# Fewer tiles projected ahead of the attention loop, the rest as side steps, and joined query DMAs

## What is computed

```python
q = split_heads(x @ wq.T) * qk_scale
k = split_heads(x @ wk.T) * qk_scale
v = split_heads(x @ wv.T)
q, k = (_rope(q), _rope(k))
energy = jnp.einsum('bhtd,bhld->bhtl', q, k) + mask
attn = jax.nn.softmax(energy, axis=-1)
out = jnp.einsum('bhtl,bhld->bhtd', attn, v)
```

## Time and profile before

| what | us |
|---|---|
| median of 3 runs | 2142.7 (2142.36 to 2144.84) |
| the profiled execution's own time | 2145.87 |
| its span, first to last instruction | 2144.1 |
| PE busy in the span | 1853.9 (86%) |
| DVE busy | 1308.9 (61%) |
| ACT busy | 975.8 (46%) |
| POOL busy | 798.0 (37%) |

### The profile page before, as it was taken

One profiled execution on the slowest core, in us unless ns is written; L12 is line 12 of the kernel. 1 busy time (PEld: TensorE's weight loads), 2 busy tenths in 40 slices (PEclk: granted clock), 3 DMA queues, 4 the chain that ended last, 5 costly groups with the idle time before them and its releaser, 6 DMA issues. The chain is left out here.

```text
span 2144.1 us, 38575 instructions
## 1 busy us (share of the span) xinstructions
PE 1853.9 (86%) x12834; PEld 1660.0 (77%) x12834; DVE 1308.9 (61%) x2935; ACT 975.8 (46%) x2165; POOL 798.0 (37%) x983
## 2 busy tenths in 40 slices
PE   5899999999999999999999995521669999999980
PEld 4688888888888888888888884511669999999980
DVE  5466654577663677663667743677856565666645
ACT  2244344344343444444443442243546666666646
POOL 3242043431142431243431101000656666766643
PEclk9799999999999999999999997555789999999995
DMA  4443134333234432234432211300024444544419
GB/s 113 113 105 99 53 99 110 99 103 95 65 96 111 105 103 81 73 92 116 102 96 78 69 50 47 136 0 0 1 79 134 152 144 156 152 154 144 147 32 313
DMA packets 189208, 215.24 MB, mean 100 GB/s; under 512 B 26672, under 2 KB 154664, under 8 KB 184964
## 3 DMA queue, kind: packets, MB, share of 16 engines
q1 hardware_dynamic: 173188, 203.12, 31.3%
q0 software_dynamic: 15872, 10.24, 2.9%
HBM read 129.66 MB, written 56.62 MB: 87 GB/s over the span
## 5 line engine op out<-in xcount | busy, mean ns | idle before, releaser
L572 PEld LDWEIGHTS out_ps<-v_sb,probs 128*128 128x128 f32 x4352 | 565.3, 193 | 20.8
L572 PE MATMUL out_ps<-v_sb,probs 128*128 128x65 f32 x4352 | 573.9, 271 | 0.0
L784 DVE TENSOR_REDUCE part_max<-rows_ps 128x1 f32<-128x512 f32 (+2 forms) x576 | 346.6, 618 | 183.3 <-PE rows_ps L531 113.2
L686 ACT ACTIVATE probs<-scores_ps 128x512 f32<-128x512 f32 (+3 forms) x640 | 329.4, 537 | 152.4 <-PE scores_ps L559 76.6
L1566 PE MATMUL up_ps<-xe_t,w 128*128 128x320 f32 x1920 | 289.7, 311 | 1.7 <-DVE xe_t L1673 1.7
L1566 PEld LDWEIGHTS up_ps<-xe_t,w 128*128 128x128 f32 x1920 | 284.6, 189 | 2.2 <-issue 1.9
L555 PE MATMUL scores_ps<-q,k_st 128*128 128x512 f32 (+2 forms) x640 | 272.9, 426 | 2.8 <-ACT probs L686 1.3
L528 PE MATMUL rows_ps<-k_st,q 128*128 128x512 f32 (+3 forms) x640 | 249.5, 404 | 22.2 <-DMA q<-q_low_cols 10.3
L960 POOL TENSOR_TENSOR products<-qk,cos_sin 128x256 f32<-128x256 f32 x236 | 169.5, 751 | 241.8 <-ACT qk L653 241.8
L556 PE MATMUL scores_ps<-q,k 68*128 68x512 f32 (+2 forms) x640 | 236.0, 369 | 0.0
L1529 POOL DMA_INDIRECT acc_rows<-out_rows,token x96 | 148.7, 1549 | 128.7 <-ACT out_rows L1656 117.4
(11 more groups left out here) (276 smaller groups left out, 2731.5 us busy)
## 6 DMA issues: line engine op xcount, KB each, us to landing
w_raw<-in_w_expert SPq DMA_DIRECT2D x32, 1536.0 KB, 6.3
k<-k_st SPq DMA_DIRECT2D x160, 128.0 KB, 2.3
k_st<-parts SPq DMA_DIRECT2D x128, 128.0 KB, 2.4
q<-q_up_cols SPq DMA_DIRECT2D x128, 128.0 KB, 2.8
w_raw<-in_w_adapter SPq DMA_DIRECT2D x32, 384.0 KB, 6.9
x_t<-in_x_t SPq DMA_DIRECT2D x64, 128.0 KB, 2.3
q_up_cols<-parts SPq DMA_DIRECT2D x64, 128.0 KB, 2.4
q_low_cols<-parts SPq DMA_DIRECT2D x64, 128.0 KB, 2.4
```

The source lines that it names most:

```text
L572: mm = pe.matmul(o_ps[:, u % 2, s * (HD + 1):(s + 1) * (HD + 1)], probs[:, g % P_RING, s * P:(s + 1) * P], v_sb[:, place(b, j), h, :], sta ...
L686: act.activation(probs[:, g % P_RING, low:CH], s_ps[:, g % S_RING, low:CH], ACT.Exp).then_inc(exp_done, 1)
L784: red = dve.tensor_reduce(to, r_ps[:, e % R_RING, 0:width], AX.X, ALU.max, negate=g == 0)
```

## The change

`FIRST` becomes 6, and all six rotations of the opening are DVE's. Tiles 6 and 7 become side steps of the loop: their inputs are loaded and split in the opening (`FIRST_X` = 8), their projections stand in slots 0 and 2, their rotation on POOL, their transposes in slots 4 and 6; the tiles behind them move to later slots, and the plan allows a tile's split only once the values of the tile two ahead are projected. The maxima of the fifth unit (the first that needs tiles 4 to 7) move from slots 1 to 8 to slots 8 to 12. The weight splits for the later projections go from behind tile 1 to the front of DVE's listing, and POOL no longer waits for the weights before its first split. In SP's listing two loads more stand ahead of each store. The two query stores of a tile are one DMA, and the two copies of a unit's upper queries are loaded by one DMA, whose source names the 64 rows twice.

```diff
-FIRST = 8
-FIRST_ON_POOL = (1, 4, 7)
+FIRST = 6
+FIRST_X = FIRST + 2
...
+        if n < FIRST_X:
+            project_at[n] = 2 * (t - FIRST)
+        elif b == 0:
+            project_at[n] = 4 + 9 * (t - 8) // 2 if t < 12 else 22 + 9 * (t - 12)
...
-                for part_, to in enumerate(("q_up", "q_low")):
-                    sp.dma_start(dram[to][:, :, n * P:(n + 1) * P].rearrange("h d t -> d h t"),
-                                 raw(parts[0:HD, n % 2, part_])).then_inc(qk_stored[n % 2], 16)
+                sp.dma_start(dram["q"][:, :, :, n * P:(n + 1) * P].rearrange("a h d t -> d a h t"),
+                             raw(parts[0:HD, n % 2])).then_inc(qk_stored[n % 2], 16)
...
-                for to in (q1[0:HD, r], q1[HD:P, r]):
-                    sp.dma_start(raw(to), dram["q_up"][h, :, tokens]).then_inc(q_loaded[r], 16)
-                sp.dma_start(raw(q2[0:HD, r]), dram["q_low"][h, :, tokens]).then_inc(q_loaded[r], 16)
+                sp.dma_start(raw(q1[:, r]), dram["q"][0, h, :, tokens].unsqueeze(0).to_broadcast([2, HD, CH]))\
+                  .then_inc(q_loaded[r], 16)
+                sp.dma_start(raw(q2[0:HD, r]), dram["q"][1, h, :, tokens]).then_inc(q_loaded[r], 16)
...
-            for n in range(2, FIRST + 2):
+            for n in range(2, FIRST_X):
                 load_xt(n)
-                if n >= 4:
-                    store_qk(n - 4)
+                if n >= 5:
+                    store_qk(n - 5)
             for u in range(HEADS):
+                if FIRST_X - 5 + u < FIRST:
+                    store_qk(FIRST_X - 5 + u)
                 load_q(u)
                 load_k2(u)
-                if u < 2:
-                    store_qk(FIRST - 2 + u)
```

More of the change, by code:

```diff
@@ L89, in attention_plan, with pieces_of @@
     pieces = [[(c, s) for c in range(blocks[u] // GROUP) for s in range(GROUP)] for u in range(len(units))]
+    def pieces_of(u):
+        return [("max", u, c, s) for c, s in pieces[u]]
     stream = [[] for _ in range(total + 1)]
@@ L101, in attention_plan @@
         begins[u] = max(slot, -1)
[L102 to L111, removed]
+    first_pieces = ((0, 0, 0, 0), (2, 2, 3, 3), (5, 5, 6, 6), (8, 9, 9, 10, 10, 11, 11, 12))
+    first_turns = (1, 4, 8, 13)
+    before = [*pieces_of(0), ("turn", 0)]
+    stream = [[e for e in now if e[1] > HEADS] for now in stream]
+    assert not stream.pop(0)
+    for u, (slots, turn) in enumerate(zip(first_pieces, first_turns), 1):
+        for e, at in zip(pieces_of(u), slots, strict=True):
             stream[at].append(e)
-            begins[u] = min(begins[u], at)
+        stream[turn].append(("turn", u))
+        begins[u] = slots[0]
     for now in stream:
@@ L133, in attention_plan @@
         finish_at.append(at)
-    chains = [(project_at[n], n, (("xt", 0, False), ("proj", 3, True), ("rope", 0, False), ("v", 1, True),
-                                  ("turn", 3, True)))
-              for n in range(FIRST, COUNT)]
+    chains = []
+    for n in range(FIRST, COUNT):
+        load = (("xt", 0, False), ("proj", 3, True)) if n >= FIRST_X else (("proj", 0, True),)
+        chains.append((project_at[n], n, load + (("rope", 0, False), ("v", 1, True), ("turn", 3, True))))
     for i in range(COUNT):
@@ L141, in attention_plan @@
         chains.append((finish_at[i], i, steps + ((("hidden", 2, True),) if i % 2 else ())))
-    after = {"proj": ("rope", 1), "ot": ("wo", AT_RING), "wo": ("x1", ROW_RING), "x1": ("x1t", ROW_RING),
+    after = {"xt": ("v", 2), "proj": ("rope", 1), "ot": ("wo", AT_RING), "wo": ("x1", ROW_RING), "x1": ("x1t", ROW_RING),
              "x1t": ("hidden", 1)}
@@ L251, in keys_stored @@
             for last in (n - 1, n):
-                eng.wait_ge(qk_stored[last % 2], 64 * (last // 2 + 1))
+                eng.wait_ge(qk_stored[last % 2], 48 * (last // 2 + 1))
         s_ps = ctx.enter_context(nc.psum_tensor("scores_ps", [P, S_RING, CH], F32))
@@ L428, in _ @@
                 turned = made.get(("turn", b * NT + GROUP * g + GROUP - 1), -2)
-                assert turned + 3 < begins[u] or u < 2 * HEADS
+                assert turned + 2 < begins[u] or u <= HEADS
                 if u >= HEADS:
@@ L761, in _ @@
             dve.wait_ge(weights_loaded, 16 * 6)
+            split(*halves(w_o), w_raw[:, W_O:W_R1])
+            split(*halves(w_r1), w_raw[:, W_R1:W_R1S])
+            dve.tensor_copy(w_r1s[:], w_r1s_raw[:]).then_inc(weights_split, 1)
+            dve.drain()
+            low = slice(STAT_COLS, 2 * STAT_COLS)
+            dve.tensor_tensor(w_r1s[low], w_r1s_raw[low], raw(w_r1s[low]), ALU.subtract).then_inc(weights_split, 1)
+            dve.drain()
+            dve.memset(v_sb[:, :, :, HD:HD + 1], 1.0).then_inc(ones_set, 1)
             rope(0)
             for n in range(FIRST):
-                if n + 1 < FIRST and n + 1 not in FIRST_ON_POOL:
+                if n + 1 < FIRST:
                     rope(n + 1)
                 lower(r_ps[:, n % 2, :], n)
[L767 to L775, removed]
             def maximum(u, c, s):
@@ L900, in lower_xt @@
                     .then_inc(xt_split, 1)
[L902 to L914, removed]
-            pool.wait_ge(weights_loaded, 16 * 6)
[L916 to L924, removed]
+            for n in range(FIRST_X):
+                lower_xt(n)
+            pool.wait_ge(weights_loaded, 16 * 6)
             def main(g):
@@ L932, in step @@
                 elif kind == "proj":
-                    products_of(k)
+                    pool.wait_ge(qk_copied, k + 1)
+                    if k > FIRST:
+                        pool.wait_ge(*at_banks(roped_ready, k - 1))
+                    rope_products(pool, cos_sin, qk[:, k % 2], products, k % NT).then_inc(rope_mul[k % 2], 1)
                 elif kind == "rope":
-                    sums_of(k)
+                    pool.wait_ge(*at_banks(rope_mul, k))
+                    pool.wait_ge(qk_turned, k - 1)
+                    rope_sums(pool, products, roped[:, k % 2]).then_inc(roped_ready[k % 2], 1)
                 elif kind == "wo":
@@ L1798, in build @@
     dram["hidden"] = nc.dram_tensor("hidden_cols", (HID, T), F32).ap()
-    for name in ("q_up", "q_low"):
-        dram[name] = nc.dram_tensor(f"{name}_cols", (HEADS, HD, T), F32).ap()
+    dram["q"] = nc.dram_tensor("q_cols", (2, HEADS, HD, T), F32).ap()
     with ExitStack() as ctx:
```

8 lines of the change are left out of this document (3 added, 5 removed).

## The result

The changed kernel takes 2206.5 us (median of four runs, 2191.27 to 2209.34), against 2143.4 for the kernel before: a ratio of 1.028, 95% interval 1.025 to 1.031. The prediction was 2143, in a range of 2128 to 2160. Its slower rival stood at 2194.

A forecast was written before the change was run, and what follows sets the result against it. PE was taken to bound the attention loop, and engines waiting in turn the opening. 2145.87 - 3.1 (up to slot 16) + 3 (loop) = 2145.8, 3.2 less for the median: 2142.6, or 2143; range 2128 to 2160.

The forecast's parts named there:

- slower rival: Query loads: two engines at 7.7 us a load, the loop losing 48 us; 2194 us, chance 0.12.
- The opening, removed: Before the loop: earlier PE start and a looser ring of stores and loads; first queries issued at 33.0, now 53.14.
- The joined load: Upper queries' load: two engines move 256 KB in 5.5 us, landing in 7.3; first product at about 40.3, against 57.37.
- The 1.8 us: Joined load's landing apart from moving bytes: a 128 KB DMA's 2.3 us less 0.5 of moving.
- The first slots: Up to slot 16: tiles 6 and 7 add 6.4 us, fifth unit's queries come at 80.8; slot 16 at 102.7, gain 3.1.
- The loop: 58 query loads from the seventh unit on: PE waits at 5.5 us a load, 3 us lost.
- The prediction's own sign of being wrong: In the loop: PE waiting for queries throughout would show the prediction wrong; few such waits were expected.
- The first one: Joined load served by all 16 engines: first product at 36.6, gain between 1 and 16.5, 13 taken; 2130 us, chance 0.26.

The follow-up runs named there:

- e2: The kernel before with one change alone, a unit's upper queries loaded by one DMA that reads the 64 rows twice: 2210.8 us.
- e4: The changed kernel, joined loads kept, with each query load eight slots ahead of its unit's first maxima in place of five: 2170.5 us.
- e10: The changed kernel, joined loads kept, with query loads eight slots ahead in place of five and tile 11 projected earlier: 2158.4 us.
- e1: The changed kernel with a unit's upper queries again loaded by two DMAs of 64 rows each: 2143.5 us.
- e3: The changed kernel with one 256 KB load from 128 distinct rows at equal steps, the upper part being stored twice: 2143.6 us.
- e5: The changed kernel with two loads of 64 rows and tiles 9 to 11 projected earlier, so tile 11 turns in slot 22: 2137.6 us.
- e11: The changed kernel with its joined load reading two separate stored copies of 64 rows, nothing read twice: 2228.4 us.
- e12: The changed kernel with its joined load reading four separately stored pieces of 32 rows, so its source counts 4 outermost: 2202.0 us.

## Why the prediction was wrong, point by point

**The opening, removed: right.** PE starts at 8.46 (8.6 predicted), tile 0's rotation at 12.05 (12.3), tile 3's lower part is done at 28.85 (29.3), and the first queries are issued at 33.4 (33.0). These rows of after are the opening's ends:

```profile
33.41 0.58 SPq L373 DMA_DIRECT2D q<-q_cols  x1
...
42.95 0.44 PE L531 MATMUL rows_ps<-k_st,q 128*128 128x128 f32 x1 [10.49 <-DMA q<-q_cols]
...
76.29 0.54 SPq L373 DMA_DIRECT2D q<-q_cols  x1
...
85.67 0.80 PE L531 MATMUL rows_ps<-k_st,q 128*128 128x512 f32 x1 [12.66 <-DMA q<-q_cols]
```

**The joined load: the mechanism right, a term too small.** Two engines, at about 25 GB/s each: 256 KB at that rate take 5.2 us, 5.5 predicted. But from the issue to the first product it takes 9.5 us (33.41 to 42.95), not 7.3. The 1.8 us that I took for all else came from the landing of a `k2` load; measured, that term is 4.3. In the DMA view of the first unit's load (window 33.4 to 43.4, 0.25 us a slice) the flat run at 49 GB/s ends at 42.15, 8.7 us after the issue, and PE starts 0.8 later:

```profile
GB/s 0 0 0 0 0 25 8 0 16 49 74 74 66 86 61 135 225 348 322 215 285 299 330 330 264 180 127 53 49 49 49 49 49 49 49 29 25 43 43 43
```

Bytes move from 1.2 us after the issue, but few at first; why, no run here tells. The earlier trace rows pointed to a larger term: three loads took 4.2 us from issue to product, and their bytes, 384 KB at 377 GB/s, only 1 of it.

**The first slots: the chain right, its length not.** The fifth unit's first product came at 85.67 for 80.8, of which 2.1 us are the load's term, and 2.8 that its issue came late (76.3 for 73.5); PE idled 12.66 us for about 10. Slot 16 came at 108.87 for 102.7. This would have made 6 us.

**The loop: the step that failed.** I took 3 us for the loop, from a load of 7.3 us and with a wait priced at its length. Both terms were too small. The trace of before gives the lead of each of the 58 loads, from its issue to the unit's first product; the tightest has 6.8 us. Taken one by one, with no load held up by another, a load of 7.3 us comes too late in two of them, by 0.9 us in all; one of 9.5 us comes too late in 20, by 21.5 us in all. e2, the joined load on that kernel, waits 20.3 us, and after 23.6. So the term of 1.8 us, which is 4.3, made the waits; I looked for the point at which two engines' throughput gives out, and e4 and e10 show that an earlier issue removes the waits with the same throughput. And in this loop a wait costs the half clock behind it as well: 88.7 us at 0.50 in after. I charged the cold clock after the opening's stall (3 us) and nothing in the loop. The prediction's own sign of being wrong, PE waiting for queries throughout the loop, is what the trace shows.

**The rivals.** The slower one named the right sign, place and nearly the size (2194), but its number is near by luck: it has loads of 7.7 us held up behind each other and 48 us of waits, where the flat runs have the rate of 5.2 us, the waits are 23.6 us, and 30 to 37 us are the clock's, which it did not price. The first one, all 16 engines at 2130, has its own test in e1 and e3: 2143.5. I had counted the tile work that each later tile brings, but had not followed tile 11, which the change turns five slots later, to the unit that waits for it in slot 32. With that mended (e5) the profiled execution takes 2132.5 and the median 2137.6.

**What is better than both kernels**: two loads of 64 rows with tile 11 in its old place, 2137.6 us, 0.24% below the kernel before.

## What to carry to other kernels

Read a DMA's outermost count before its bytes: joining two loads into one that counts 2 saved one issue of 0.6 us and put 256 KB on two engines, at 46 to 54 GB/s. Compare a load's whole time from issue to use, not its moving time, with the lead of each single use, and follow every step that was moved to the first one that waits for it. Where PE runs at full clock without a gap, price a wait at its length and half of the time at 0.50 behind it (the table's stretches, less what of them lies inside the waits). For after, e1, e3, e11 and e12 against e5, and for e2 against before, that comes to 2 to 6% more than slots 16 to 600 lost, for e4 to 8% less.

## What was not expected of the hardware

At or after a single wait of PE in a full loop (1.36 us long at 461.5 in after, 1.8 in e10, 9.1 in slot 32 of after) the clock went to 0.50 for 3.4 to 23.9 us, most of it with PE at work: 20.00 of 20.00 us in after. Not each wait does it: of e2's ten waits of 0.9 to 2.4 us in the loop four were followed by such a stretch. Which ones do, and what ends such a stretch, no run here tells.

SP pays for narrow loads as well. Where several joined loads are under way, the issue behind them lasts 3.94 and 5.46 us (the rows at 384.12 and 389.38) instead of 0.5, and everything behind it in SP's order comes later by that. In e12, with four pieces, no issue of a query load lasts longer than 0.94 us.
